# A bidirectional WKV scan with a sign-weight projection: signs made on ScalarE, a product schedule a step ahead, one residual DMA per step

## The reference, cut to what matters

```python
tf    = sigmoid(sum(cond))                       # one value a batch
decay = exp(-exp(w)) * (0.5 + 0.5 * tf)          # per channel and batch
ek, ekv = exp(min(k, 30)), exp(min(k, 30)) * k
# first-order recurrences over time, forward and backward, of ekv (num) and ek (den)
num = nf + nb - ekv + exp(min(u + k, 30)) * k
den = df + db - ek  + exp(min(u + k, 30))
y   = sigmoid(x) * num / max(den, 1e-8) * (0.8 + 0.2 * tf)
bw  = where(weight >= 0, 1, -1) * mean(|weight|, axis=1)
out = x + einsum('bsi,oi->bso', y, bw) + bias
```

## Time and profile before

| | |
|---|---|
| runs | 534.94, 535.40, 535.63 us, median 535.4 |
| the profiled execution | 534.87 us, its span 533.0 us |
| mean granted PE clock of it | 0.839 of full speed |
| busy, share of the span | DVE 94%, POOL 72%, ACT 71%, PE 69%, PEld 40% |
| DMA | 92.65 MB, mean 174 GB/s |

### The profile page before, as it was taken

How to read it: one execution, slowest core, us unless ns; L and a number is a source line. 1 busy time by engine, 2 the same in 40 slices (tenths; PEclk the granted TensorE clock), 3 DMA queues, 4 the chain that set the end, 5 groups by cost and what they waited for, 6 DMA issues and landing times.

```text
span 533.0 us, 5373 instructions
## 1 busy us (share of the span) xinstructions
PE 368.3 (69%) x1803; PEld 212.0 (40%) x1803; DVE 501.9 (94%) x378; ACT 378.9 (71%) x415; POOL 385.1 (72%) x202
## 2 busy tenths in 40 slices
PE   2333323322396787796978777877988998698997
PEld 1233313312243444443534444444444555354443
DVE  4999999999999999999999999999999999998593
ACT  2858768595868969696969789696979799683100
POOL 0469888988866777887788777778877978776200
PEclk9997565555588798879789787988799999799999
DMA  6755777787545888888889998887888999983943
GB/s 187 208 140 176 176 202 194 178 236 182 134 118 119 168 164 162 170 179 184 182 178 193 197 189 162 165 160 175 183 190 173 188 267 152 198 169 79 181 174 119
DMA packets 125923, 92.65 MB, mean 174 GB/s; under 512 B 2860, under 2 KB 117576, under 8 KB 125896
## 3 DMA queue, kind: packets, MB, share of 16 engines
q0 software_dynamic: 30720, 33.56, 39.9%
q1 hardware_dynamic: 93096, 57.70, 36.8%
q10 hardware_dynamic: 2080, 1.05, 0.7%
HBM read 58.74 MB, written 16.78 MB: 142 GB/s over the span
## 4 chain that ended last, share of the span: by engine, by line
DVE 64%; issue 19%; PE 8%; POOL 3%; DMA 3%; SPq 1%; ACT 1%; DVEq 0%; ACTq 0%; POOLq 0%
DVE pair L677 23%; DVE pair L691 13%; DVE pair L704 7%; DVE wkv L721 7%; DVE own L705 6%; DVE pair L701 4%; DMA y_fm<-in_L_ffn_weight_dram 3%; PE sT L411 3%; DVE euk L726 2%; PE kT L411 2%; PE yT L411 1%; PE kT L354 1%; POOL o_nat L286 1%; POOL wkv L329 1%; DVE y_start L683 1%
## 5 line engine op out<-in xcount | busy, mean ns | idle before, releaser
L376 PE MATMUL prod<-acts,sgn 128*128 128x512 f16 x768 | 197.1, 415 | 4.8 <-ACT orow L612 3.1
L691 DVE TENSOR_TENSOR_SCAN pair<-cols,y_start,pair 128x1024 f32<-128x1024 f32 x64 | 150.1, 2346 | 1.3 <-DVE y_start L683 0.2
L677 DVE TENSOR_TENSOR_SCAN pair<-cols,pair 128x1024 f32<-128x1024 f32 x64 | 142.8, 2272 | 0.0
L376 PEld LDWEIGHTS prod<-acts,sgn 128*128 128x128 f16 (+1 forms) x768 | 81.5, 106 | 102.7 <-issue 32.6
L354 PE MATMUL kT<-ident,k_nat 128*128 128x128 f32 x256 | 46.6, 342 | 76.4 <-DVE own L705 76.4
L329 POOL TENSOR_TENSOR wkv<-wkv,rec 128x1024 f32<-128x1024 f32 x31 | 73.4, 2369 | 34.4 <-ACT wkv L585 34.4
L548 ACT ACTIVATE rec<-euk,lnb 128x1024 f32<-128x1024 f32 x32 | 36.8, 1149 | 77.7 <-DVE euk L726 77.7
L319 POOL TENSOR_TENSOR wkv<-euk,rec 128x1024 f32<-128x1024 f32 x31 | 78.1, 2518 | 9.1 <-ACT rec L550 9.1
L336 POOL TENSOR_TENSOR wkv<-wkv,pair 128x1024 f32<-128x1024 f32 x31 | 73.1, 2357 | 8.6 <-DVE wkv L721 8.3
L279 POOL TENSOR_TENSOR acts<-wkv,rec 128x1024 f16<-128x1024 f32 x31 | 74.0, 2387 | 4.6 <-ACT rec L559 4.6
L354 PEld LDWEIGHTS kT<-ident,k_nat 128*128 128x128 f32 x256 | 37.9, 178 | 83.3 <-issue 83.3
(11 more groups left out here) (89 smaller groups left out, 535.7 us busy)
## 6 DMA issues: line engine op xcount, KB each, us to landing
x_nat<-in_x_dram SPq DMA_DIRECT2D x32, 512.0 KB, 6.0
pair<-own POOLq DMA_DIRECT2D x32, 512.0 KB, 4.6
k_nat<-in_fside_BxSxS_dram SPq DMA_DIRECT2D x30, 512.0 KB, 4.3
o_nat<-in_x_dram POOLq DMA_DIRECT2D x24, 512.0 KB, 6.2
out_dram<-o_nat SPq DMA_DIRECT2D x24, 512.0 KB, 5.4
y_fm<-in_L_ffn_weight_dram SPq DMA_DIRECT2D x8, 512.0 KB, 8.4
x_end<-in_x_dram SPq DMA_DIRECT2D x6, 512.0 KB, 8.6
x_end<-in_L_ffn_bias_dram POOLq DMA_DIRECT2D x6, 512.0 KB, 8.8
```

Source lines behind the costliest of these rows:

```text
L376: ins = pe.matmul(prod[:, h, :], view[:, c, m % CT * P:m % CT * P + P], acts[:, part, m // CT % 2 * CT + c, h * H:(h + 1) * H], start=(par ...
L677: dve.tensor_tensor_scan(buf, d, buf, 0.0, ALU.mult, ALU.add).then_inc(st["F" + kind], 1)
L691: dve.tensor_tensor_scan(buf[:, ::-1], d, buf[:, ::-1], y_start[:, i:i + 1], ALU.mult, ALU.add)\
```

## The change

ScalarE makes the signs: `Sign(w * 2^24 + 2^-126)`, directly behind the absolute sums, and the copy behind the transpose multiplies by 0.5. POOL's `signs` is gone. The table of units is new: steps 19 and 21 make three units, steps 23 and 22 two, step 24 none of its own but most of units 32 and 33, step 25 the rest of these and two more, steps 26 to 29 three each, so the last unit, 47, is made in step 29 (before: 30). `added` lets one residual DMA go per step and never two, so residual m goes in step m + 11 throughout: before, m = 16 and 17 went in step 27, 19 and 20 in step 29, 21 in 30, 22 in 31 and 23 behind the loop; now m = 19 goes in step 30, 20 in 31, and 21, 22, 23 behind the loop. SP's stores of a step stand at the end of its own step and no longer at the start of the next. ACT evacuates units 41, 42, 43 in step 28, 44, 45, 46 in step 29 and 47 in step 30, ahead of `two`; `y_copy(47)` moves from step 31 into step 30. Three outputs of batch 3 (8, 9, 10) are begun early, in step 30, over four channel tiles, and their partial sums are saved there. What the engines' programs lose or gain, cut to the core:

```diff
-    LATE = {N - 7: 35, N - 6: 38, N - 5: 41, N - 4: 44, N - 3: 46}
+    MORE = {19: 23, 20: 25, 21: 28, 22: 30, 23: 32, 24: 32, 25: 36, 26: 39, 27: 42, 28: 45}
     def made(n):
-        return 0 if n < LAG else LATE.get(n, 2 * LAST) if n > N - CT else 2 * (n - LAG + 1)
+        return 0 if n < LAG else 2 * LAST if n > N - 4 else MORE.get(n, 2 * (n - LAG + 1))
     def cleared(n):
-        return 0 if n < LAG else made(n) - 1 if n < N - 2 else 2 * LAST
+        return 0 if n < LAG else 2 * LAST if n >= N - 2 else made(n) if made(n) == made(n - 1) else made(n) - 1
-    copied[2 * LAST - 1] = N - 1
+    copied[2 * LAST - 1] = N - 2
+    added = [0]
+    for m in range(LAST):
+        added.append(max(copied[2 * m + 1], added[-1]) + 1)
     def summed(n):
-        return [m for m in range(LAST) if copied[2 * m + 1] + 1 == n]
+        return [m for m in range(LAST) if added[m + 1] == n]
...
 # SP, step
-                stores(n - 1)
...
+                stores(n)
...
 # POOL, step
-                    residuals(summed(n)[:1])
-                if wt:
-                    done(pool, "clamp", n)
-                    signs(n, p)
+                    residuals(summed(n))
...
-                residuals(summed(n)[1:])
...
 # PE, step
+                if n == N - 2:
+                    done(pe, "ev", 2 * LAST - 2)
+                    done(pe, "lo", N - 5)
+                    across(0, bank[0], range(CT - 4), True, False)
+                    turned(2 * LAST - 1)
+                    across(8, bank[1], range(CT - 4), True, True).then_inc(st["early"], 1)
+                    done(pe, "yc", 2 * LAST - 1)
+                    across(9, bank[4], range(CT - 4), True, True).then_inc(st["early"], 1)
+                    pe.wait_ge(st["early_sb"], 1)
+                    across(1, bank[1], range(CT - 4), True, False)
+                    pe.wait_ge(st["early_sb"], 2)
+                    across(10, bank[4], range(CT - 4), True, True).then_inc(st["early"], 1)
...
 # PE, tail
-            turned(2 * LAST - 1)
-            across(1, bank[1], range(CT - 3), True, False)
...
-            done(pe, "yc", 2 * LAST - 1)
-            across(8, bank[4], range(CT - 3), True, True).then_inc(st["early"], 1)
+            pe.wait_ge(st["early_sb"], 3)
+            across(4, bank[4], range(CT - 3), True, False)
             done(pe, "lo", N - 3)
-            for v in range(4):
+            for v in range(5):
                 across(v, bank[v], range(CT - 3, CT - 2), False, False)
             s_turn(N - 1)
-            pe.wait_ge(st["early_sb"], 1)
-            across(9, bank[4], range(CT - 2), True, True).then_inc(st["early"], 1)
             done(pe, "yd", N - 1)
             across(5, bank[5], range(CT - 2), True, False)
-            pe.wait_ge(st["early_sb"], 2)
-            across(4, bank[4], range(CT - 2), True, False)
...
-                tiles = range({6: CT - 1, 7: CT - 1, 8: CT - 3}.get(v, CT - 2) if v < 10 else 0, CT)
+                tiles = range(CT - 2 if v < 6 else CT - 1 if v < 8 else CT - 4 if v < 11 else 0, CT)
...
 # ACT, step
                 if n == N - 1:
-                    y_copy(2 * LAST - 1)
+                    early_out(2)
                 if mid:
                     done(act, "chk", n - 1)
                     act.activation(wkv[1 - p][:, :], ...)
+                if n == N - 2:
+                    y_copy(2 * LAST - 1)
                 if nxt:
                     exps(n + 1, 1 - p)
+                if n == N - 2:
+                    early_out(0)
+                    early_out(1)
...
+                    done(act, "wT", n - 2)
+                    act.activation(s_nat[p], w_nat[p][:, :], ACT.Sign, scale=TINY_GAIN, bias=tiny[:, 0:1])\
+                       .then_inc(st["sgn"], 1)
...
-                    act.activation(sgn[:, :, n * P:(n + 1) * P], wT, ACT.Identity, bias=shift[:, 0:1]).then_inc(st["wTc"], 1)
+                    act.mul(sgn[:, :, n * P:(n + 1) * P], wT, SIGN).then_inc(st["wTc"], 1)
...
 # DVE, tail
-                if v in (8, 9):
-                    dve.wait_ge(st["early_sb"], 2)
+                if 8 <= v <= 10:
+                    dve.wait_ge(st["early_sb"], 3)
```

More of the change, by code:

```diff
@@ L36 @@
 SIGN = 0.5
+TINY = 2.0 ** -126
+TINY_GAIN = 2.0 ** 24
 SEED = 2
@@ L103, in bi_wkv_binary_ffn @@
         junk = o_nat[2][:, :, :].rearrange("p q f -> p (q f)")
-        early_part = [y_fm[0][:, h * H:(h + 1) * H] for h in range(NH)]
+        early_part = [y_fm[0][:, 0:H], y_fm[0][:, H:T], y_fm[1][:, 0:H]]
         s_nat = [o_nat[p][:, 0:TT // 2, :].rearrange("p q f -> p (q f)").bitcast(F16) for p in range(2)]
@@ L129, in bi_wkv_binary_ffn @@
         two = sb("two", [P, 1])
-        shift = sb("shift", [P, 1])
+        tiny = sb("tiny", [P, 1])
         kT = ps("kT", [P, T])
@@ L249, in step @@
                     load_tail(TT - N + n)
+                stores(n)
             out_ = out
             run(step)
-            stores(N - 1)
-            stores(N)
+            for n in range(N, added[-1] + 1):
+                stores(n)
             for q in range(TT - 1):
@@ L269, in _ @@
         def _(pool):
-            seed(pool, "chk", "inv", "base", "lo", "sgn")
+            seed(pool, "chk", "inv", "base", "lo")
             pool.memset(ident[:, :], 1.0).then_inc(s_id, 1)
@@ L280, in low_half @@
                     .then_inc(st["lo"], 1)
[L282 to L286, removed]
             def biases(q):
@@ L342, in _ @@
             low_half(N - 2, 0)
-            residuals(summed(N))
+            for n in range(N, added[-1] + 1):
+                residuals(summed(n))
             biases(TT - 2)
@@ L379, in product, with part @@
                 return ins
[L381 to L385, removed]
+            def part(u, lo, hi):
+                done(pe, "lo", u // (2 * CT) * CT + hi - 1)
+                if lo == 0:
+                    done(pe, "ev", u - 2)
+                product(u, range(lo, hi))
             def rest(u):
@@ L426, in step @@
             def step(n, p, wt, nxt, nxt3, mid, low, out):
+                units = list(range(made(n - 1), made(n)))
                 first = n % CT == 1 and n >= LAG
[L428 to L431, removed]
-                    unit(units[0])
-                if mid and n < N - 1:
+                ahead = n == LAST
+                split = units[0:2] if first else ()
+                if first and n != LAST + 1:
+                    part(units[0], 0, CT - 1)
+                elif units and not first:
+                    unit(units[0])
+                if n == N - 1:
+                    done(pe, "lo", N - 4)
+                    for v in (0, 1):
+                        across(v, bank[v], range(CT - 4, CT - 3), False, False)
+                if mid:
                     s_turn(n - 1)
@@ L436, in step @@
                     k_turn(n + 1, 1 - p)
[L437 to L442, removed]
+                if ahead:
+                    for u in (made(n), made(n) + 1):
+                        part(u, 0, CT - 2)
+                    for u in (made(n), made(n) + 1):
+                        part(u, CT - 2, CT - 1)
+                if first and n != LAST + 1:
+                    part(units[1], 0, CT - 1)
                 if first:
-                    most(units[1])
                     rest(units[0])
@@ L447, in step @@
                     turned(u - 1)
-                for i, u in enumerate(units[1:]):
-                    if first and i == 0:
+                for u in units[1:]:
+                    if u in split:
                         rest(u)
@@ L500, in _ @@
         def _(act):
-            seed(act, "expE", "expU", "sig", "ln", "rec", "two", "hi", "hib", "ev", "yc", "abs", "wTc")
+            seed(act, "expE", "expU", "sig", "ln", "rec", "two", "hi", "hib", "ev", "yc", "abs", "sgn", "wTc")
             act.dma_start(k_nat[0][:, :, :], tile_of(k, 0)).then_inc(k_in[0], 16)
@@ L516, in exps @@
                 act.activation(ek[p], kT[:, :], ACT.Exp).then_inc(st["expE"], 1)
-                act.activation(euk[p][:, :], kT[:, :], ACT.Exp, bias=ucol[:, bass.ds(n, 1)])\
+                act.activation(euk[p][:, :], kT[:, :], ACT.Exp, bias=ucol[:, n:n + 1])\
                    .then_inc(st["expU"], 1)
@@ L563, in early_out @@
                 act.wait_ge(st["early"], i + 1)
-                act.copy(early_part[i], bank[4]).then_inc(st["early_sb"], 1)
+                act.copy(early_part[i], bank[1 if i == 0 else 4]).then_inc(st["early_sb"], 1)
             act.wait_ge(s_const, 4)
@@ L594, in step @@
                     done(act, "abs", n - 1)
-                    act.activation(junk, w_nat[p][:, :], ACT.Abs, accum_out=asum[:, bass.ds(n, 1)])\
+                    act.activation(junk, w_nat[p][:, :], ACT.Abs, accum_out=asum[:, n:n + 1])\
                        .then_inc(st["abs"], 1)
+                    done(act, "wT", n - 2)
+                    act.activation(s_nat[p], w_nat[p][:, :], ACT.Sign, scale=TINY_GAIN, bias=tiny[:, 0:1])\
+                       .then_inc(st["sgn"], 1)
```

(3 more changed lines are left out.)

10 lines of the change are left out of this document (4 added, 6 removed).

## The result

The changed kernel takes 540.62 us (median of 4, 540.41 to 541.67) against 535.32 for the one before: ratio 1.0103, interval [1.0086, 1.0121], so slower by 1%. That is inside the range of 532 to 542.5 and 2.4 us above the forecast of 538.2. The profiled execution took 540.41 us with a span of 538.7, 5.7 above the span of before. The code moved some lines: L701 is now L717, L721 L737, L726 L742, L536 L546, L585 L595, L329 L323, L336 L330, L548 L558, L298 L297, L221 L226; also L319 is now L314, L279 L284, L354 L349, L376 L371 and L411 L407. The other kernels of the experiments are shifted by a few lines in the same way.

The account below looks back on a forecast made before the run. DVE was taken to bound the kernel, busy 94% of the span, PE the tail. 534.87 - 4.6 + 5.65 + 1.8 = 537.7 us profiled, 538.2 us as a median; range 532 to 542.5 for 8 in 10.

Parts of the forecast that it names:

- Bound and rule: All steps: DVE bounds them; `two` may start 5.43 us after the clamp, each further microsecond lengthening the step by one.
- Signs: Steps 2 to 7: moving signs from POOL to ACT removes their excess, -4.6 us, ends -5.0 and -3.5.
- The 0.4 given back in steps 3, 5 and 7: ACT 0.73 us late after even steps against 0.61 slack, so 0.12 lost in each of three steps.
- One residual DMA a step: Step 30: m = 23's copy waits for m = 19's store ahead of `two`, +5.65 us, ends +5.2 and +9.
- the second DMA cost nothing: Steps 27 and 29: their excess is ACT's lateness, not the second residual DMA; removing it brings 0.
- The rest of step 30: ACT and PE work behind the late copy makes step 31's Ln late: +1.8 us, ends 0 and +3.6.
- Batch 2 a step sooner: Three units in steps 19 and 21; ACT's extra evacuations fall in odd steps without tables: 0 us.
- cover gone: Case where the extra PE unit's delay of `exps` is not hidden: 0.5 us in steps 20 and 22.
- an excess in steps 19 to 25: Sign that the forecast is wrong: steps 19 to 25 running long, which it priced at nothing.
- Tail: After the last step: PE's earlier start, -0.9 us, against a slower-clock restart: 0 us, ends -0.9 and +1.3.
- the end of +1.3: Tail's unfavourable end, if PE idles and restarts at the lower clock: +1.3 us.
- the price of a restart: Tail: PE restarting at the lower clock after idling costs up to 2.2 us.

Follow-up runs that it names:

- one residual alone: The kernel before with only the residual rule changed, residual m going in step m + 11, table of units as before: 535.32 us against 534.75, ratio 1.0001.
- residual by copy: The changed kernel with the earlier residual rule, each sent the step after its second half is copied, two a step where due: 534.00 us against 534.76, ratio 0.9989.
- copy behind exps: The changed kernel with step 30's evacuation of unit 47 and waiting copy put behind `two` and the exponentials on ACT: 540.72 us against 534.76, ratio 1.0095.
- Three in 25: The changed kernel with another table of units: three in step 25, three in 26, four in 27; 540.45 us in one run.
- signs undone: The changed kernel with the signs back on POOL and ACT's `Sign` out: 546.77 us against 534.42, ratio 1.0203.
- tail filled: Residual by copy, with PE's matmuls of output 4 over six channel tiles moved behind output 5's, into the tail's idle stretch: 532.26 us against 534.75, ratio 0.9946.

## Why the prediction held, and which term failed

**Bound and rule.** That DVE bounds the steps, and that `two` may start 5.43 us after the clamp with each further microsecond lengthening the step, held in each kernel: `two` at 6.76, 8.03 and 11.25 was 1.33, 2.60 and 5.82 late, and the steps were 1.30, 2.56 and 5.75 over.

**Signs: -4.6 forecast, -4.9 measured.** All the excess of steps 2 to 7 was that of POOL's signs. The 0.4 given back in steps 3, 5 and 7 did not come: in step 5 `two` started at 88.04, 5.51 after the clamp, and the step took 14.73; the slack is 0.1 wider than worked out.

```profile
88.04 1.15 ACT L595 ACTIVATE wkv<-wkv,two 128x1024 f32<-128x1024 f32 x1 [0.44 <-POOL wkv L314]
```

**One residual DMA a step: +5.65 forecast, +5.75 measured.** The round trip was as worked out: issue at 1.04, store at 7.33 (forecast 7.2), copy at 10.76 (10.6). That the second DMA cost nothing, and that it takes the moved copy as well to make the wait, is shown by one residual alone and residual by copy; copy behind exps shows that a copy moved forward waits wherever it stands in the step.

**The rest of step 30: +1.8 forecast, +1.6 measured.** In step 31 `two` started 7.13 us after the clamp, 1.7 late. PE's turn of unit 47 took 1.09 us and the first 8 matmuls 3.52, at the lower clock level, the next 8 1.89:

```profile
467.51 1.09 PE L349 MATMUL yT<-ident,y_fm 128*128 128x128 f32 x4 [5.42 <-ACT o_nat L546]
468.39 3.52 PE L407 MATMUL prod<-sgn,acts 128*128 128x512 f16 x8
471.75 1.89 PE L407 MATMUL yT<-sgn,acts 128*128 128x512 f16 x8
```

**Batch 2 a step sooner: 0 forecast, +3.8 measured.** This is the term that was mis-sized, and the main reason for the 2.4 us between forecast and result; signs and tail came out 1.0 us better than forecast and hid a part of it. The step of the working that failed is "ACT's extra evacuations fall in odd steps, which have no tables": I counted ACT's load, but not when PE can hand it the units. In step 25, PE could not begin until the low part of tile 23 was there,

```profile
385.43 1.04 PE L371 MATMUL prod<-acts,sgn 128*128 128x512 f16 x2 [3.02 <-POOL acts L284]
...
388.97 4.02 PE L371 MATMUL prod<-acts,sgn 128*128 128x512 f16 x16
...
393.26 3.62 PE L371 MATMUL prod<-acts,sgn 128*128 128x512 f16 x16
...
401.48 1.04 PE L349 MATMUL kT<-ident,k_nat 128*128 128x128 f32 x8
```

7.4 us into the step, and two full units, of 4.02 and 3.62 us, were left behind it. The third evacuation therefore waited past the step's end (1.30), and the fourth unit pushed the turn of k in step 26, to 8.7 us after the clamp against 4.3 before (2.00 more than the 0.56 that step 27 had before). Three in 25 shows that the fourth unit carries it. How much it costs varies with PE: in the five profiles with this table through step 25, step 26 took 15.17, 15.76, 15.95, 16.01 and 16.42 us, and the first of the two full units 3.62, 3.97, 3.95, 4.02 and 4.42. The granted clock was 0.50 from 384 to 388 us here; that a faster clock alone would have made step 26 shorter is argued and not tested. Step 21's 0.49 is the same on a small scale: ACT waited 1.00 us for k in step 20. I had priced that wait at 0.5 and under "cover gone"; it came in the profiles of four of the six kernels with this table up to step 24 (0.2 to 0.5 us in step 21), and in one of the others as 0.26 in step 23. The prediction named an excess in steps 19 to 25 as a sign that it is wrong, and step 21 shows one.

**Tail: 0 forecast, -0.7 measured**, inside its ends of -0.9 and +1.3. PE idled for 1.72 us ahead of the 28 matmuls and did them in 6.20. That is partly luck: signs undone has the same tail, idled for 3.39 us there and took 48.7 us, 2.2 over before. Copy behind exps and residual by copy had 48.8 and 48.6. So the end of +1.3 was too near: I had taken the price of a restart from one row as 2.2 us, and the matmuls took up to 2.9 more.

## What to carry to other kernels

A buffer's users should be traced through every engine: that a step later for one DMA is free depends on where the next user's wait stands, and it can become a wait of a whole round trip (9.7 us from issue to the free buffer here) ahead of something on the bound engine's path; putting the wait elsewhere on the same in-order queue helped only where everything with a due time stood ahead of it. When units of work are moved to "idle" slots, list for each slot when its input is there and what stands behind it on the producer, and not only the consumer's load. And of a change in several parts each part should be timed alone: here one part gives 4.9 us, and the others together take 10.6 in the profiles.

## What was not expected of the hardware

The level of TensorE's clock in the tail moved its length more than the matmuls' number did. The same 28 matmuls of 128x512, by the idle stretch ahead of them and the granted clock of about their first 6 us:

| kernel | idle, us | 28 matmuls, us | granted clock |
|---|---|---|---|
| after | 1.72 | 6.20 | 1.00 |
| tail filled | 2.84 | 7.61 | 0.76 |
| three in 25 | 3.21 | 7.56 | 0.77 |
| copy behind exps | 3.32 | 9.14 | 0.50 |
| signs undone | 3.39 | 9.06 | 0.51 |
| residual by copy | 4.79 | 9.00 | 0.55 |

The Trainium skill (TensorE: Matmul & The Clock Gate, Part 1) says that the engine runs at 1.2 GHz after idleness and at 2.4 GHz once it has been busy; the traces agree in the last three rows, with 0.50 to 0.55 of full speed. So where PE ran ahead of its inputs before the PE-bound tail, up to 2.9 us of what was won was lost again.

The changed kernel and signs undone have the same tail program and differ in the idle stretch all the same. Ahead of it, the eight transposes of the last sigmoid took 1.91 us in the changed kernel and 1.04 in signs undone, and the matmuls beside them were slower in the changed kernel too:

```profile
493.78 1.91 PE L349 MATMUL sT<-ident,x_nat 128*128 128x128 f32 x8
```

So PE was through with the work ahead of the idle stretch later, idled less, and made the 28 matmuls at full clock. Why the clock came back earlier in one execution than in the other, no run here shows.
